# AdaLN block with local attention: value products in quarters of the array, a mask by 64-row products, statistics from plain transposes, new orders on four engines

## The reference

```
for i in range(6):
    x = attn_layer(shift_tokens(x), Wqkv[i], ...) + x     # 16 heads of 64, windows of 32
    x = ffn_layer(shift_tokens(x), ...) + x               # norm, 128 -> 2*341, gelu gate, 341 -> 128
```

## Time and profile before

| what | us |
|---|---|
| median of three runs | 3455.47 |
| the profiled execution, its own time | 3455.64 |
| its span | 3453.9 |
| TensorE busy | 3233.1 (94%) |
| VectorE busy | 3171.4 (92%) |
| GpSimd busy | 2706.3 (78%) |
| ScalarE busy | 2438.2 (71%) |
| value products with all keys (L624), busy | 379.8 |
| products for the window before (L631), busy | 94.5 and 94.5 |
| statistics products (L652), busy | 55.1 |
| mask products (L604), busy | 73.0 |

### The profile page before, as it was taken

How to read it: one execution, slowest core, us unless ns; L and a number is a source line. 1 busy time by engine, 2 the same in 40 slices (tenths; PEclk the granted TensorE clock), 3 DMA queues, 4 the chain that set the end, 5 groups by cost and what they waited for, 6 DMA issues and landing times.

```text
span 3453.9 us, 108159 instructions
## 1 busy us (share of the span) xinstructions
PE 3233.1 (94%) x45916; PEld 2089.8 (61%) x46108; DVE 3171.4 (92%) x2914; ACT 2438.2 (71%) x3945; POOL 2706.3 (78%) x1265
## 2 busy tenths in 40 slices
PE   5657999999999999999999999999999999999996
PEld 3325666666666666666666666666666666666663
DVE  6759999999999999999999999999999999999992
ACT  4645777777777777777777777777777777777764
POOL 4547888888888888888878888888888888888871
PEclk9889999999999999999999999999999999999996
DMA  2001111122111122111122111112211122211111
GB/s 77 2 0 32 40 42 39 40 55 57 38 44 39 39 53 57 41 42 42 38 52 54 47 39 41 42 51 52 50 39 40 42 52 51 49 41 39 41 41 39
DMA packets 150433, 148.32 MB, mean 43 GB/s; under 512 B 39228, under 2 KB 95424, under 8 KB 149952
## 3 DMA queue, kind: packets, MB, share of 16 engines
q1 hardware_dynamic: 149952, 141.39, 16.6%
HBM read 19.62 MB, written 2.10 MB: 6 GB/s over the span
## 4 chain that ended last, share of the span: by engine, by line
PE 38%; DVE 26%; ACT 12%; issue 10%; POOL 5%; SPq 2%; DMA 1%; ACTq 0%; DVEq 0%; POOLq 0%
PE bank L574 11%; PE bank L673 7%; DVE rot L1405 6%; PE mid L583 4%; DVE rot L1411 4%; DVE raw L1397 4%; PE mid L624 4%; PE bank L644 4%; DVE Pr L1369 4%; PE mid L611 4%; ACT sq L911 3%; POOL FX L1164 3%; ACT mid L944 3%; DVE mx L1347 2%; ACT raw L903 2%
## 5 line engine op out<-in xcount | busy, mean ns | idle before, releaser
L574 PE MATMUL bank<-wqkv,xs 128*128 128x512 f32 x2304 | 1133.0, 605 | 11.0 <-ACT raw L903 8.5
L1145 POOL TENSOR_TENSOR rr<-ssm,nhalf 128x32 f32<-128x32 f32 x192 | 1051.8, 5478 | 16.0
L1155 POOL TENSOR_TENSOR swp<-raw,TS 128x1024 f32<-128x1024 f32 x384 | 896.8, 2356 | 175.1 <-DVE raw L1397 175.1
L903 ACT ACTIVATE raw<-bank 128x512 f32<-128x512 f32 x768 | 447.5, 598 | 424.2 <-PE bank L574 258.4
L574 PEld LDWEIGHTS bank<-wqkv,xs 128*128 128x128 f32 x2304 | 394.4, 191 | 310.4 <-issue 267.2
L1397 DVE TENSOR_TENSOR raw<-raw,rr 128x2048 f32<-128x2048 f32 x192 | 489.9, 2552 | 16.8 <-POOL rr L1145 16.8
L1391 DVE TENSOR_REDUCE ss<-sq 128x16 f32<-128x1024 f32 x384 | 463.5, 1207 | 23.7 <-ACT sq L911 12.1
L583 PE MATMUL mid<-ident,rot 128*128 128x128 f32 x3072 | 416.6, 279 | 52.0 <-DVE rot L1411 23.1
L583 PEld LDWEIGHTS mid<-ident,rot 128*128 128x128 f32 x3072 | 336.9, 142 | 204.1 <-ACT OT L950 134.6
L1411 DVE TENSOR_TENSOR rot<-rot,swp 128x2048 f32<-128x2048 f32 x192 | 440.1, 2292 | 21.1 <-DVE rot L1405 1.4
L1405 DVE TENSOR_TENSOR rot<-raw,TC 128x2048 f32<-128x2048 f32 x192 | 434.1, 2261 | 0.0
(11 more groups left out here) (134 smaller groups left out, 4443.8 us busy)
## 6 DMA issues: line engine op xcount, KB each, us to landing
PT<-PTd SPq DMA_DIRECT2D x1344, 64.0 KB
xs<-F SPq DMA_DIRECT2D x192, 64.0 KB, 1.9
wqkv<-d_wqkv SPq DMA_DIRECT2D x36, 256.0 KB, 3.3
VT<-V SPq DMA_DIRECT2D x144, 64.0 KB
BT<-PTd SPq DMA_DIRECT2D x288, 32.0 KB
fwo<-d_fwo SPq DMA_DIRECT2D x6, 512.0 KB, 4.1
d_out<-X SPq DMA_DIRECT2D x8, 256.0 KB, 2.3
w<-d_w SPq DMA_DIRECT2D x6, 341.0 KB
```

What stands on the lines that cost most here:

```text
L574: nc.tensor.matmul(bank[bk][:, :], xs[:, j, :], wqkv[:, c, :], start=True, stop=True)\
L903: nc.scalar.activation(raw[:, j % 2, c * 512:(c + 1) * 512], bank[RAW_BANK[c]][:, :], ACT.Copy)\
L1145: pool.tensor_tensor(rr[:, :], ssm[:, :], nhalf[:, :], ALU.pow).then_inc(rr_ready, 1)
L1155: last = pool.tensor_tensor(dst[:, :, :, t, :], src[:, :, :, 1 - t, :], tab.unsqueeze(2).broadcast_to([P, 2, HEADS, 32]), ALU.mult)
```

## The change

What it does, part by part:

- **Value products.** `pv` becomes `pv_first` and `pv_second`. The product of 128 keys with 128 queries becomes one of the lower 64 keys with the first 96 queries (`low_keys`) and one of the upper 64 keys with the last 64 queries (`high_keys`). The products for the window before (`keys_in_front`) take 64 rows, of which 32 hold zeros (`BT` and `VT` are cleared at the start). Consecutive products go to different row halves and different banks. A new semaphore `pv_half` is raised behind `pv_first`; `to_v` and the `VT` move wait for it instead of `pv_done`. The part of `VT` and `BT` used is now partitions 0 to 63 for the first four head pairs.
- **Mask.** Instead of one product with a 128 x 128 identity per bank, the first bank's mask uses array rows 0 to 63 and the second's rows 64 to 127: a table of 33 pattern rows is picked by `pickb`.
- **Statistics.** `centred` transposes the plain rows (no `cen`); `ffn_rstd` on GpSimd also makes -mean and -mean/std (`nmr`), and `ffn_normed` on ScalarE applies it as the bias (Identity instead of Copy). `cen` is no longer loaded.
- **Orders.** On all four engines and on SyncE. TensorE: `proj` 1, 3, 0, 2 in place of 1, 0, 3, 2 (banks 0, 1, 0, 1; the weight loads likewise), `scores` from the slot's front with lag 3 to its end with lag 2, the gated and linear FFN products in another order. ScalarE: `squares 0` behind `exps`, `o_to_sbuf` ahead of `squares 1`, `to_v` behind the q/k copies, `attn_to_sbuf` one slot earlier, the gelus at the end of slot 1. GpSimd: the third `gated` ahead of `sin_part`. VectorE: see the diff. SyncE: the Wo load one tile's moves earlier, and the `VT` move for `pv_half`.
- The loop runs `slots(4)` in place of `slots(8)`, which leaves out turns that hold nothing.

```diff
-        RAW_BANK = (1, 0, 1, 0, 0, 1)
+        RAW_BANK = (0, 0, 1, 1, 0, 1)
...
             def bands(n, j):
 
+                if j > 0:
+                    wait(sp, pv_half, n)
+                    sp.wait_ge(v_out[0], n)
+                    sp.dma_start(VT[0:W, :], V[P - W:P, 1 - j % 2, 0:512]).then_inc(band_moved, 16)
                 wait(sp, pv_done, n)
-                if j > 0:
-                    sp.wait_ge(v_out[1], n)
-                    sp.dma_start(VT[P - 2 * W:P - W, :], V[P - W:P, 1 - j % 2, 512:1024]).then_inc(band_moved, 16)
                 sp.wait_ge(pT_ready, n + 1)
...
                 for h in range(2):
                     if h == 1:
                         pe.wait_ge(qkT_out[LAST_QK], n + 1)
-                    nc.tensor.matmul(bank[3 + h][:, :], identb[:, :],
-                                     maskb[:, 1 if j == 0 else 0, :, :].rearrange("p h k -> p (h k)"),
+                    r = slice(h * DH, (h + 1) * DH)
+                    nc.tensor.matmul(bank[3 + h][:, :], pickb[r, :],
+                                     maskb[r, 1 if j == 0 else 0, :, :].rearrange("p h k -> p (h k)"),
                                      start=True, stop=False, skip_group_check=True)
...
+            def low_keys(j, u, h, start):
+                hc = (2 * u + h) * DH
+                return nc.tensor.matmul(OUT_BANK[u // 4][h * DH:(h + 1) * DH, (u % 4) * P:(u % 4) * P + 3 * W],
+                                        V[0:DH, j % 2, hc:hc + DH], PT[0:DH, 0:3, h * HH + u, :],
+                                        start=start, stop=True, skip_group_check=True)
+
+            def high_keys(j, u, h, start):
+                hc = (2 * u + h) * DH
+                return nc.tensor.matmul(OUT_BANK[u // 4][h * DH:(h + 1) * DH, (u % 4) * P + 2 * W:(u % 4 + 1) * P],
+                                        V[DH:P, j % 2, hc:hc + DH], PT[DH:P, 2:4, h * HH + u, :],
+                                        start=start, stop=True, skip_group_check=True)
+
+            def keys_in_front(j, u, h, start):
+                hc = (2 * u + h) * DH
+                r = slice(0, DH) if u < 4 else slice(DH, P)
+                nc.tensor.matmul(OUT_BANK[u // 4][h * DH:(h + 1) * DH, (u % 4) * P:(u % 4) * P + W],
+                                 VT[r, hc:hc + DH] if u < 4 else V[r, 1 - j % 2, hc:hc + DH], BT[r, h * HH + u, :],
+                                 start=start, stop=False, skip_group_check=True)
+
+            def pv_first(n, b, j):
...
+                if j > 0:
+                    for u in range(4):
+                        for h in range(2):
+                            keys_in_front(j, 4 + u, h, u == 0)
+                            keys_in_front(j, u, h, u == 0)
+                for u in range(4):
                     for h in range(2):
+                        high_keys(j, 4 + u, h, j == 0 and u == 0)
+                        mm = low_keys(j, u, h, j == 0 and u == 0)
+                mm.then_inc(pv_half, 1)
...
+                for u in range(4):
+                    for h in range(2):
+                        high_keys(j, u, h, False)
+                        mm = low_keys(j, 4 + u, h, False)
                 mm.then_inc(pv_done, 1)
...
                 for t in range(TPB):
-                    mm = nc.tensor.matmul(bank[7][:, t * P:(t + 1) * P], FX[:, t * P:(t + 1) * P], cen[:, :],
-                                          start=True, stop=True)
+                    mm = nc.tensor.transpose(bank[7][:, t * P:(t + 1) * P], FX[:, t * P:(t + 1) * P], ident[:, :])
                 mm.then_inc(cen_done, 1)
...
             def to_v(n, b, j, c):
                 act.wait_ge(proj_done[c], n + 1)
-                wait(act, pv_done, n)
+                wait(act, pv_half, n)
...
-                pool.tensor_tensor(rstd[:, :], vpe[:, :], nhalf[:, 0:TPB], ALU.pow).then_inc(rstd_ready, 1)
+                pool.tensor_scalar(nmean[:, :], mv[:, :, 0], -1.0, None, ALU.mult).then_inc(mean_ready, 1)
+                pool.tensor_tensor(rstd[:, :], vpe[:, :], nhalf[:, 0:TPB], ALU.pow).then_inc(rpow_ready, 1)
+                pool.wait_ge(rpow_ready, b + 1)
+                pool.wait_ge(mean_ready, b + 1)
+                pool.tensor_tensor(nmr[:, :], rstd[:, :], nmean[:, :], ALU.mult).then_inc(rstd_ready, 1)
```

386 lines of the change are left out of this document (193 added, 193 removed).

## The result

The changed kernel took 3465.09 us, the median of 13 runs (3459.05 to 3467.48), against 3456.03 us for the kernel before on the same chips (13 runs, 3451.93 to 3457.74). The ratio is 1.0023 with a 95% interval of 1.0015 to 1.0031: slower by 9 us. The forecast was 3417, faster by 38: the time lies within the stated range of 3335 to 3530, but on the other side of the kernel before.

The account below looks back on a forecast made before the run. VectorE's own order was taken as the bound. A batch was 60.9 + 1.2 statistics + 2.05 FFN slots + 0.2 plain slots = 64.3 against 65.1 us, saving 38 us over 48 batches: 3417 us, range 3335 to 3530.

Parts of the forecast that it names:

- exp in the slot of the table load: ScalarE, second FFN slot: exp done at 15.3 against 14.0 wanted; slot 1.3 us late, first squares another 0.1.
- ScalarE's Identity with a bias instead of Copy: FFN norm on ScalarE: the bias in place of a plain copy costs nothing, being off the chain.
- Value products: TensorE: 2.50 us a tile falls to 2.05 with four quarters, within bounds of 1.8 and 3.0.
- rival D: Weight loads overlap only across row groups: value products 4.2 us, about 70 us a batch, 3690 us; chance 0.04.
- The added wait of the second squares: ScalarE: squares now stand behind value products and output copy; 0.2 us a batch in plain slots, 0.25 in first FFN slot.
- VectorE is the bound: VectorE's instructions follow without a hole, 15.47 us for a tile without FFN extras; anything above that is its stalls.
- rival C: Loop of transpose, band moves, value products, output copy, second squares and second sum becomes the bound; 3547 us, chance 0.19.
- The prediction had seen the second loop: ScalarE's chain less-max, exp, copy, squares, as tight as VectorE's own; a wait of 0.17 us in three of four slots.
- GpSimd's two instructions: Mean for the statistics on GpSimd: +0.5 to +1.3 us a batch, covered by 3.2 us spare, so costs nothing.
- VectorE's new order: VectorE, probabilities and transpose apart: 15.22 us a plain tile, 60.9 for four, plus 1.2 for statistics.
- The mask: TensorE, two 64-row products for two of 128 rows: gain between -0.1 and 0.3 us, taken 0.15.
- rival B: Nothing net: value products stay at 2.5 us, each FFN slot 0.45 later, 65.2 a batch, 3455 us; chance 0.12.

Follow-up runs that it names:

- Experiments 2: Changed kernel with exp ahead of the third linear copy on ScalarE and the third gate product back behind the sine part on GpSimd; 3438.55 us, ratio 0.9951.
- 8: Changed kernel with tanh in place of gelu, so no table loads, and a result that is not the reference's; 3418.39 us, ratio 0.9889.
- experiment 11: Changed kernel with Copy and scale in place of Identity with bias in the FFN norm, mean not taken off; 3448.23 us, ratio 0.9977.
- experiment 4: Changed kernel with the old value products, everything else as changed; 3488.10 us, ratio 1.0093.
- experiment 5: Changed kernel with the first gate product of the FFN moved behind the value products in the first FFN slot; 3462.66 us, ratio 1.0020.
- experiment 6: Kernel before with the sum of exponentials over 32 of 64 keys, which changes the softmax; 3447.29 us, ratio 0.9971.
- Experiment 13: Changed kernel with exp ahead of the third linear copy, the third gate product behind the sine part, and the old statistics; 3419.51 us, ratio 0.9892.

## Why the prediction was wrong, point by point

The forecast can be added up by slots from its own terms: 15.47 for slot 0 (15.22 + 0.25), 17.02 for slot 1 (15.22 + 1.4 + 0.4), 15.32 for slot 2 and 16.52 for slot 3 (15.22 + 0.1 each, 1.2 for the statistics in the last), together 64.33. Measured are 15.85, 17.43, 15.40 and 16.63, together 65.31. The difference is 0.98 us a batch, 47 us over 48 batches, and so the whole distance between a gain of 38 and a loss of 9. It lies in slot 1 (0.41) and slot 0 (0.38), with 0.08 and 0.11 in the other two. Two terms failed: exp in the slot of the table load, which was sized too small, and the bias of the FFN norm, which was put at nothing.

- *exp in the slot of the table load.* Forecast: the slot ends 1.3 us late, the first squares 0.1 more, the second sum of the tile after 0.4. Measured: the sum of exponentials 1.97 late, and 0.17 at each of the two places behind it, 2.31 in all against 1.8. The gelus of slot 0 waited for TensorE (1.60 us before one of them), whose FFN products stood behind the scores, and the linear copy and exp came behind the gelus. Experiments 2 and 8 show the place: 26.5 and 47 us.
- *"ScalarE's Identity with a bias instead of Copy ...: nothing, each off the chain."* This is the step that failed outright. It is 0.1 us on each of four instructions, ahead of transposes, affine, FFN products, value products and second squares, and cost 17 us (experiment 11); 0.28 of slot 0's 0.38 is this. It alone turned a gain of 0.2% (0.9977) into a loss of 0.2%.
- *Value products.* Taken 2.05, measured 2.26; the mechanism held (four quarters work side by side), and rival D, the strict reading of row groups with 4.2 us, fell. By experiment 4, where 0.23 to 0.25 us cost 23 us, the missing 0.21 would be worth some 20 (an estimate; it overlaps with the other terms).
- *The added wait of the second squares.* The place was right. The wait was 0.87 us in slot 0 of the batch shown, where 0.08 and 0.25 stood, 0.29 in slot 2, where 0.08 and 0.1 stood, and about 0.17 in slots 1 and 3, where it had 0.4 and 0.18. The cause was not the one of the sum: it had the value products start at the landing of the band DMAs, 7.9 us behind the transpose, and they started at 8.6, when TensorE came to them. So it is not rival C's loop through the band moves. In slot 0 it is TensorE's line ahead of the value products: with one FFN product moved behind them (experiment 5) the slot fell by 0.60.
- *"VectorE is the bound."* Half right. In a plain slot of the kernel before, 12.81 of the 15.48 us are VectorE's in either loop, but the sum of exponentials is not among them: experiment 6 took 0.53 us a tile from it and got 0.05 back. The prediction had seen the second loop ("as tight as VectorE's own") and used it only as a correction of 0.17 us. This did not make the forecast wrong by itself, since the terms above account for it.
- *GpSimd's two instructions, "it costs nothing".* As far as the runs can tell this is right (3.9 us, not clear of noise), but not for the reason given. There is spare before the user and none before the cosine part: the power starts 0.06 us ahead of it, and where it comes behind it lasts 2.1 us longer.
- *VectorE's new order.* A plain slot was 15.40 in place of 15.22, and before 15.48. FX and the normalising product came as forecast or better (2358 against 2559 ns). *The mask:* taken 0.15; its record starts 0.32 us ahead of the scores where it was 0.37, and no run varied it alone.

That the time came out near rival B (3455) is no merit of B: it rested on value products that stay at 2.5 us, and they fell to 2.26. Experiment 13 gave 45.6 us by moving exp and dropping the bias, but the forecast had itself allowed for a late exp, so this is what was to be had there and not a measure of its error. Open: why the changed kernel took 3459 us in two of 13 executions and 3460.6 to 3467.5 in the others. The collisions do not explain it, since they cost nothing in the trace. The two short ones had a mean clock of 0.978 and the others 0.976 or 0.977; each kernel has one trace, so it stays open.

## What to carry to other kernels

When one engine runs without a hole, take a known piece of work from it before you believe that it is the bound: a second loop of the same length leaves no idle time to see. Choose the piece with care, for such a loop can share most of the engine's instructions, and only those beside it are free. Then look at each kind of slot by itself, since they need not have the same bound. Price an instruction by what waits behind it in its own slot, not by its engine's idle share; 0.1 us on four copies ahead of a long line costs as much as a large rearrangement gains. When work is hurried or delayed on an engine that shares memory with another, look at what it will start beside, and whether the time lost there was spare.
